# Later keys of the diagonal attention tiles: mask products on TensorE replaced by a select on GpSimd

## The reference, cut to what matters

```
x = x + attn_a(norm(x)); x = x + ffn(norm(x)); x = x + attn_b(norm(x)); x = x + ffn(norm(x))

attn_b:  q = concat(x @ Wq1, x @ Wq2) in 32 heads of 32;  k, v in 16 heads, each used by two q heads
         scores = q k^T / sqrt(32), later keys (key > query) set to the lowest float
         y = softmax(scores) v;   y = y1 - sigmoid(x @ Wlam) * y2;   return y @ Wo
```

## Time and profile before

| | |
|---|---|
| runs | 2116.13 us median of 3 (2113.49 to 2116.81) |
| profiled execution | span 2112.1 us from first to last instruction; no time of its own is given, so the runs' 2113.49 to 2116.81 us stand for it |
| PE busy | 2028.2 us (96%) |
| DVE busy | 1288.4 us (61%) |
| POOL busy | 879.5 us (42%) |
| ACT busy | 856.5 us (41%) |
| attention | about 760 to 1746 us of the span |

### The profile page before, as it was taken

One profiled execution on the slowest core, in us unless ns is written; L12 is line 12 of the kernel. 1 busy time (PEld: TensorE's weight loads), 2 busy tenths in 40 slices (PEclk: granted clock), 3 DMA queues, 4 the chain that ended last, 5 costly groups with the idle time before them and its releaser, 6 DMA issues.

```text
span 2112.1 us, 29403 instructions
## 1 busy us (share of the span) xinstructions
PE 2028.2 (96%) x11783; PEld 901.3 (43%) x11824; DVE 1288.4 (61%) x1854; ACT 856.5 (41%) x1307; POOL 879.5 (42%) x457
## 2 busy tenths in 40 slices
PE   8998999999999999999999999999999889899999
PEld 3444444444444445343434434343433334444444
DVE  5868687747755734455555555555557664775634
ACT  4534353335434322434443434434443442443431
POOL 3756585600000001667666666766666681000000
PEclk9999999999999999999999999999999999999999
DMA  7111110300000011000100010000000021000001
GB/s 234 35 33 33 30 36 30 115 30 1 1 1 1 1 49 26 1 16 11 21 11 21 1 27 5 16 16 11 6 11 6 18 73 40 1 0 21 21 1 40
DMA packets 68999, 55.53 MB, mean 26 GB/s; under 512 B 36800, under 2 KB 55232, under 8 KB 68608
## 3 DMA queue, kind: packets, MB, share of 16 engines
q1 hardware_dynamic: 61952, 41.07, 6.7%
q10 hardware_dynamic: 6912, 12.59, 1.9%
HBM read 43.02 MB, written 10.62 MB: 25 GB/s over the span
## 4 chain that ended last, share of the span: by engine, by line
PE 53%; DVE 4%; ACT 3%; POOL 2%; issue 1%; DVEq 0%; ACTq 0%; POOLq 0%
PE psum L128 9%; PE psum L1198 8%; PE psum L1288 8%; PE psum L1349 6%; PE psum L152 5%; PE psum L1332 5%; PE psum L1236 3%; PE psum L1328 2%; PE psum L1294 2%; PE psum L1306 2%; DVE b_maxima L1642 2%; POOL b_totals L1579 2%; PE psum L1319 1%; PE psum L1246 1%; ACT b_probs L1499 1%
## 5 line engine op out<-in xcount | busy, mean ns | idle before, releaser
L1579 POOL TENSOR_TENSOR b_totals<-b_totals,b_probs 128x2048 f32<-128x2048 f32 (+5 forms) x160 | 504.0, 3150 | 312.0 <-ACT b_probs L1499 306.0
L1642 DVE TENSOR_REDUCE b_maxima<-psum 128x2 f32<-128x1024 f32 (+3 forms) x384 | 350.6, 954 | 391.5 <-PE psum L1294 233.8
L1499 ACT ACTIVATE b_probs<-psum 128x1024 f32<-128x1024 f32 (+3 forms) x320 | 228.7, 766 | 249.6 <-PE psum L1332 233.0
L447 PE MATMUL psum<-hT,a_win 128*128 128x512 f32 x640 | 293.5, 602 | 2.6 <-DVE a_parts L751 1.2
L128 PE MATMUL psum<-hT,b_early 128*128 128x512 f16 x1024 | 228.8, 383 | 9.8 <-DVE b_middle L214 6.9
L128 PE MATMUL psum<-hT,W 128*128 128x512 f16 x1024 | 226.1, 381 | 3.7 <-DVE a_win L214 3.6
L447 PEld LDWEIGHTS psum<-hT,a_win 128*128 128x128 f32 x640 | 120.5, 193 | 131.3 <-issue 129.8
L128 PEld LDWEIGHTS psum<-hT,b_early 128*128 128x128 bf16 x1024 | 100.3, 99 | 135.7 <-issue 10.6
L128 PEld LDWEIGHTS psum<-hT,W 128*128 128x128 bf16 x1024 | 100.3, 98 | 125.3 <-DVE a_win L214 6.5
L1555 POOL MEMSET b_mask<- 128x128 f32 x1 | 0.2, 205 | 350.9 <-POOLq L279 350.9
L680 POOL TENSOR_TENSOR a_parts<-a_parts 128x512 bf16<-128x512 bf16 x48 | 60.1, 1253 | 133.4 <-DVE a_parts L754 133.4
(11 more groups left out here) (232 smaller groups left out, 3286.9 us busy)
## 6 DMA issues: line engine op xcount, KB each, us to landing
a_parts<-in_w_guT ACTq DMA_DIRECT2D x32, 256.0 KB, 2.8
ternary<-W SPq DMA_DIRECT2D x1, 6144.0 KB, 18.0
a_win<-in_w_inT SPq DMA_DIRECT2D x20, 256.0 KB, 7.8
a_parts<-in_w_pT ACTq DMA_DIRECT2D x16, 256.0 KB, 2.6
b_down<-lam_rows SPq DMA_DIRECT2D x32, 128.0 KB, 2.7
b_early<-ternary SPq DMA_DIRECT2D x8, 512.0 KB, 8.2
out<-x SPq DMA_DIRECT2D x16, 256.0 KB, 2.2
x<-in_x SPq DMA_DIRECT2D x3, 1024.0 KB, 8.0
```

Source lines behind the costliest of these rows:

```text
L447: last = pe.matmul(ring(s, j), win[:, at:at + P], core["hT"][:, (i * KT + k) * BLK:(i * KT + k + 1) * BLK], start=(k == 0), stop=(k == KT ...
L1499: act.activation(held(u, s)[:, 2 * a:2 * a + 2, off:BLK], pair_banks(("score", u, s, a))[:, :, off:BLK], ACT.Exp, scale=SCALE).then_inc(ex ...
L1579: pool.tensor_tensor(acc, acc, held(u, s)[:, own, off:BLK], ALU.add).then_inc(summed, 1)
L1642: dve.tensor_reduce(maxima[u % 2][:, :].rearrange("p (h q c) -> p h q c", h=HPT, q=QT)[:, 2 * a:2 * a + 2, qt, kc], pair_banks(("row", u, ...
```

## The change

The mask products leave `scores`; each pair is now taken just ahead of its own products, on diagonal steps too. POOL gets a new instruction per diagonal step, `drop_later`, which sets the probabilities of later keys to zero in place: all four heads, 128 queries each, so 128 x 512 elements in four pieces with a stride of 512. It stands in POOL's list ahead of that step's `add_up`. A new semaphore `masked` counts them. PE's `weigh` waits for `masked` instead of `exped` on diagonal steps, and so do the sums on POOL and DVE. The row work keeps its own mask products (L1294).

```diff
+def masked_by(u, s):
+    diagonal = [kt >= TPB * c for c, kt in STEPS]
+    return sum(diagonal) * u + sum(diagonal[:s + 1])
...
             def scores(u, s):
...
-                if diagonal:
-                    for j in range(HPT):
-                        if j % 2 == 0:
-                            to.append(take_pair(("score", u, s, j // 2)))
-                        pe.matmul(to[j // 2][:, j % 2, off:off + P], ident_b[:, :], later_key[:, :],
-                                  start=True, stop=True)
...
                 for a in range(2):
-                    if not diagonal:
-                        to.append(take_pair(("score", u, s, a)))
+                    to = take_pair(("score", u, s, a))
...
             def weigh(u, s):
...
                 for j in range(HPT):
-                    pe.wait_ge(exped, (u * NS + s) * 2 + j // 2 + 1)
+                    if diagonal:
+                        pe.wait_ge(masked, MASK_PARTS * masked_by(u, s - 1) + min(j // 2 + 1, MASK_PARTS))
+                    else:
+                        pe.wait_ge(exped, (u * NS + s) * 2 + j // 2 + 1)
...
             def add_up(u, s):
...
                 pool.wait_ge(exped, 2 * g + 2)
+                if kt >= TPB * c:
+                    pool.wait_ge(masked, MASK_PARTS * masked_by(u, s))
...
+            def drop_later(u, s):
+                off, g = step_width(s), u * NS + s
+                pool.wait_ge(exped, 2 * g + 2)
+                own = held(u, s)[:, :, off:off + P]
+                pool.affine_select(out=own, in_=own, compare_op=ALU.is_ge, fill=0.0, base=0,
+                                   pattern=[[0, HPT], [1, P]], channel_multiplier=-1).then_inc(masked, 1)
...
             for u in range(UNITS):
                 for s in range(NS):
+                    if STEPS[s][1] >= TPB * STEPS[s][0]:
+                        drop_later(u, s)
                     if STEPS[s][1]:
                         add_up(u, s)
```

More of the change, by code:

```diff
@@ L903 @@
 LEAD = NR + 2
+MASK_PARTS = 1
 HEAD_AT = [0, 2, 1, 3]
@@ L1069, in phase_rest @@
         out_done, out_added = sem("out_done"), sem("out_added")
-        shared = sem("shared")
+        shared, masked = sem("shared"), sem("masked")
         turn_ready, high_kept = sem("turn_ready"), sem("high_kept")
@@ L1312, in scores @@
                 r, w = divmod(u, 2)
-                off, diagonal = step_width(s), kt >= TPB * c
-                to = []
-                if diagonal:
-                    for j in range(HPT):
-                        if j % 2 == 0:
-                            to.append(take_pair(("score", u, s, j // 2)))
-                        pe.matmul(to[j // 2][:, j % 2, off:off + P], ident_b[:, :], later_key[:, :],
-                                  start=True, stop=True)
+                off = step_width(s)
                 if kt == 0:
@@ L1323, in scores @@
                 for a in range(2):
-                    if not diagonal:
-                        to.append(take_pair(("score", u, s, a)))
+                    to = take_pair(("score", u, s, a))
                     for j in (2 * a, 2 * a + 1):
                         rows = slice(j * HD, (j + 1) * HD)
-                        pe.matmul(to[a][:, j % 2, off:BLK], ones_b[rows, :],
-                                  bias[u % 2][rows, c * BLK + off:(c + 1) * BLK],
-                                  start=not diagonal, stop=False, skip_group_check=diagonal)
+                        pe.matmul(to[:, j % 2, off:BLK], ones_b[rows, :],
+                                  bias[u % 2][rows, c * BLK + off:(c + 1) * BLK], start=True, stop=False)
                     for j in (2 * a, 2 * a + 1):
-                        last = pe.matmul(to[a][:, j % 2, off:BLK], strip(kT[w][r % 2], j, kt * P, (kt + 1) * P),
-                                         strip(qT[w][r % 2], j, c * BLK + off, (c + 1) * BLK), start=False, stop=True,
-                                         skip_group_check=diagonal)
+                        last = pe.matmul(to[:, j % 2, off:BLK], strip(kT[w][r % 2], j, kt * P, (kt + 1) * P),
+                                         strip(qT[w][r % 2], j, c * BLK + off, (c + 1) * BLK), start=False, stop=True)
                     last.then_inc(scored, 1)
@@ L1340, in weigh @@
                 off = step_width(s)
-                first, final = kt == 0, s == CHUNK_LAST[c]
+                first, final, diagonal = kt == 0, s == CHUNK_LAST[c], kt >= TPB * c
                 if first and u * CQ + c:
@@ L1649, in share_sum @@
                 dve.wait_ge(exped, 2 * g + 2)
+                if kt >= TPB * c:
+                    dve.wait_ge(masked, MASK_PARTS * masked_by(u, s))
                 if kt == 1:
```

## The result

The changed kernel takes 2136.5 us (median of 4 runs, 2131.45 to 2137.3), the kernel before 2115.1 us: ratio 1.0099, 95% interval 1.0085 to 1.0113. It is 21.4 us slower where 8.9 us were forecast. A second measurement gave 2135.1 against 2114.9 us, ratio 1.0098 (1.0083 to 1.0113). The profiled execution took 2131.45 us with a span of 2129.6 us, 17.5 us over the span of before; it was the fastest of the four.

What follows compares the result with a forecast made beforehand. PE was taken as the bound in middle units; the masks' 28.2 us are given back to POOL's selects and 8.9 us more, so span 2112.1 becomes 2121.0 and, with the median 4.0 above it, 2125 us; range 2110 to 2146 us.

Steps and rivals of the forecast that it cites:

- What bounds the kernel: In the middle units PE is the bound; POOL is idle in each unit's first half and full in the second.
- The length of the select: On POOL, 128 x 512 elements: 0.64 us, 0.72 us in the queue; outer bounds 0.30 and 1.18 us.
- The masks' price: 512 mask products leave PE's diagonal steps: 0.22 us a step, 1.76 us a unit, 28.2 us gained if nothing replaces them.
- fewer pair waits: PE's idle time before mask products partly goes: 1.8 us gained, 0.25 us at step 3 of seven odd units.
- The queue's walk: POOL's list from step 5 to step 11 with four selects: odd units 0.7 us longer, even units 0.3 us longer.
- The sum: Odd units 4.9, even 1.8, first -1.0, last but one +1.0, last +4.0, pair waits -1.8: +8.9 us.
- The third rival: New PE stalls also lower the clock: 1.4 us lost in each odd unit and the last but one, 2136 us; chance 0.07.
- The last unit: POOL's queue is the critical path; selects delay ACT and the final weighing, about 4 us in all.
- none at steps 0 to 3: PE's weighings wait for selects only at steps 8 to 11; waits in steps 0 to 3 would show it wrong.
- Hidden selects: Short selects let POOL's tail in steps 8 to 11 end before PE needs it: faster, 2105 us at 0.30 us; chance 0.12.
- The long select: A select of 0.89 us on POOL gives 2140 us, one of 1.18 us gives 2157 us; chance 0.21.
- taken up by other waits: Pair waits and DVE's holds in late steps vanish behind the new stalls: 2114 to 2119 us; chance 0.13.

## Why the prediction was wrong

**What bounds the kernel: right.** PE in the middle, with POOL's list full from step 5 on. The kernels without selects, with shorter selects and with a lighter list show it from three sides.

**The length of the select: right.** 0.64 us forecast, 0.640 us measured. Splitting the one short row by the adds' fixed part was the right choice. That split says 0.60 us; the 0.04 us on top was a guess without a row behind it, and that it came out to the last digit is luck. The memsets' fixed part, and the 0.87 us that the Trainium skill's page (GPSIMD Engine Reference, Performance versus the Vector engine) leads to, were too long for this instruction. The bound from 0.60 to 0.89 us held.

**The masks' price: right in the middle, too high at the end.** 1.66 us a unit, 0.21 us a step, in units 1 to 12; nothing in units 13 to 15. The 1.8 us for fewer pair waits, 0.25 us at step 3 of each odd unit, do not show: without selects the odd units from 3 to 11 gained 1.54 us, less than the masks' 1.76 us, and units 7 and 9 of the kernel before have no idle time on PE at step 3. Without this term the sum would have been 10.7 us.

**The queue's walk: right in the units it was made for.** Odd units from 3 to 9 0.6 us longer (unit 11: 0.9 us) where 0.7 less a pair wait of 0.25 was said, even ones 0.35 to 0.38 us (unit 8: 0.1) where 0.3 was. The eleven units from 2 to 12 come to 5.2 us against 4.1.

**The sum carried two of the units wrongly.** The first unit was to gain 1.0 us and lost 0.6 us. The profile shows its weighings of steps 10 and 11 waiting 0.91 and 0.32 us for selects, and between them a wait that is no weighing's: PE's first bias product of the next unit waits 1.88 us for POOL's `spread`. Without selects this wait is 1.03 us.

```profile
882.78 0.41 PE L1327 MATMUL psum<-b_last_bias,b_ones_b 32*128 32x512 bf16 x4 [1.88 <-POOL b_last_bias L1563]
```

And unit 13 was counted as one more odd unit. It took 56.67 us before where the other odd units took 58.21 us, since it has fewer projections to do, while POOL's list is the same. So the same queue stands out by 1.5 us more. Its weighing of step 9 waits 4.67 us, where the other odd units wait 1.9 us:

```profile
1653.75 1.51 PE L1349 MATMUL psum<-b_probs,b_middle 128*32 128x384 f32 x8 [4.67 <-POOL b_probs L1588]
...
1656.54 3.25 PE L1313 MATMUL psum<-b_wo,b_down 128*128 128x512 f32 x4
```

**The step that failed most, by the estimate below: the clock left out of the sum.** The prediction saw the mechanism and gave it 0.07, with the ground that "the present waits of middle units leave the clock at 1.00". The new waits are longer than the present ones. Not each is followed by the lower clock: in the changed kernel's profile units 2 to 12 have waits of 1.2 to 1.9 us and stay at the full clock. The two rows above show it in unit 13: eight products that take 0.85 us in unit 7 take 1.51 us, and four output products, 1.95 us in the middle units, take 3.25 us, behind a wait of 4.67 us. The stretch (changed kernel, columns as in the earlier trace rows):

```profile
1652.00:1659.00 7.00, 5.25 (x24) 2.35 (x25) 2.25 (x7) 0.00 (x0) 6.72 (x5) 0.53 0.00 0
...
884.50:888.00 3.50, 3.50 (x18) 1.05 (x13) 0.00 (x0) 2.06 (x3) 1.85 (x2) 0.52 0.00 0
935.50:939.00 3.50, 3.48 (x22) 1.63 (x23) 0.94 (x3) 0.00 (x0) 3.39 (x2) 0.52 0.00 0
```

A granted clock of 0.52 is the lower level (1.2 GHz) over nearly the whole stretch. The second begins behind the three waits at the end of unit 0, the third in the weighing behind the 1.93 us wait at step 9 of unit 1. Unit 1 grew by 2.95 us where the next odd units grew by 0.59; with masks and selects, where it holds no such stretch, it grew by 1.52 us as the next ones did (1.51). So 6.8 us at the lower level cost 2.4 us. The Trainium skill (TensorE: Matmul & The Clock Gate, HAM oscillation) tells of waits in a loop that bring the lower clock, and for its own example counts half of the time at it as lost; the first agrees with these rows, the second is more than the 0.32 to 0.35 found here.

How much of the 21.4 us this is can be estimated in two ways, and was not measured by itself: no kernel was run in which PE waits for POOL while the clock is held up. The kernel with masks and selects comes nearest: it took 2 to 3.5 us less than the 10 us that the queue alone would add.

- By unit, from the profiled execution: 2.4 us in unit 1; about 1.7 us in unit 13 (3.79 us, less the 0.59 of an odd unit and the 1.5 that it is shorter); 1.3 us less behind the attention, which holds 4.0 us less at the lower level. That is near 3 us. This execution was the fastest; the medians are 21.4 us apart where its span is 17.5 us longer, and the 3.9 us between go with a lower mean clock. About 7 us in all. In the second measurement's profile unit 12 shows one such difference by itself: 61.89 us with 3.4 us at the lower level, 60.75 us without.
- By the mean clock. A mean clock c on a span S means 2 x (1 - c) x S at the lower level. The eight runs of the changed kernel go from 2129.6 us at 0.987 to 2135.0 us at 0.983: 17 us more at the lower level, 5.4 us more time, 0.32 us for each. The kernel before has 0.992 (34 us); the changed kernel's typical 0.9845 is 66 us. 32 x 0.32 = 10 us. This is rather too much: in the profile 12.7 us of the additional time at the lower level lie in the last unit, where PE waits for POOL at any clock.

So 7 to 10 us are the clock's and 11 to 14 us the queue's, where the sum had 8.9 us for the queue and nothing for the clock. With its first unit and unit 13 corrected (1.6 + 1.5 us) the sum has 12 us. The third rival's forecast, 2136 us, had the mechanism, but fits the measured time by luck: it put 1.4 us into each odd unit and the last but one, while the profile shows the loss in units 1 and 13 and none in 3 to 11.

**The last unit: right in size, with waits where none were said.** 4.0 us forecast, 4.6 us measured, with POOL's list as the path. But "none at steps 0 to 3" did not hold, and waits there were named as a sign of being wrong. The tightest of these steps was looked for in unit 8; in the last unit, which has no row work on PE, the weighings of steps 0, 2 and 3 wait 0.73, 1.14 and 0.66 us for selects:

```profile
1731.71 0.64 PE L1349 MATMUL psum<-b_probs,b_middle 128*32 128x256 f32 x8 [1.14 <-POOL b_probs L1588]
```

In units 0 to 14 no weighing of these steps waits for a select.

**The rivals.** Hidden selects failed on the length. It is the short select (0.296 us) that gives the faster kernel, 2111.9 us; the prediction had 2105 us for it. That is the right direction, 7 us too far. The long select failed as well; its time (2140 us) is near the measured one for another reason. The lateness was not taken up by other waits.

## What to carry to other kernels

Work moved to an engine that is busy for 71% on average can still land in the one stretch where it has no gap: walk that engine's list from its last idle time to the instruction that is waited for, for every kind of unit, the first and the last too, and count some of TensorE's clock with each new wait. Then take as much out of that stretch as is put in: one add on DVE and one take in idle time turned 1.0% slower into 1.1% faster, while reordering the list took 4 us off, since in every other unit it only moved the wait to the next buffer that the list guards.

## What the runs showed of the hardware

The select on GpSimd took 0.296 us for 128 x 128 f32 and 0.636 us (median) for 128 x 512 in four pieces: 0.34 us for 384 elements more, so 0.89 ns an element and 0.18 us fixed, where an add takes 2.12 ns and 0.20 us.

Beside some DVE instructions it took longer: in the changed kernel 0.824 us twice in unit 14, beside a DVE TENSOR_SCALAR of 128 x 512; in the kernel with the add of step 8 on DVE 1.83 to 2.11 us in seven places, beside a DVE add of 128 x 2048, which in six of them also took 3.30 us instead of 2.28 us. Beside DVE's maxima alone it kept its 0.63 to 0.64 us.

The same program came out up to 7.5 us apart in span (2125.1 to 2132.6 us), the longer ones at the lower mean clock (0.988 to 0.982). Whether a wait of 1 to 2 us is followed by the lower clock differed from unit to unit and from run to run.
